# ScalarE takes the copy of the turned first-norm row before the second norm of its step

## The reference, cut to what matters

```
h = concat(token_table[x], cat_table[x])          # 64 x 128 x 256
h = h + linear_attention(layernorm(h))            # 16 heads, phi = elu + 1
h = h + moe_attention(layernorm(h))               # 16 experts, top two, then causal attention
```

## Time and profile before

| what | value |
|---|---|
| median of three runs | 983.25 us |
| the profiled execution, its own time | 981.2 us |
| its span, first to last instruction | 979.5 us |
| mean granted TensorE clock (1.0 is full speed) | 0.996 |
| PE busy | 922.2 us, 94% of the span |
| DVE busy | 843.0 us, 86% |
| POOL busy | 675.2 us, 69% |
| ACT busy | 599.7 us, 61% |

### The profile page before, as it was taken

How to read it: one execution, slowest core, us unless ns; L and a number is a source line. 1 busy time by engine, 2 the same in 40 slices (tenths; PEclk the granted TensorE clock), 3 DMA queues, 4 the chain that set the end, 5 groups by cost and what they waited for, 6 DMA issues and landing times.

```text
span 979.5 us, 20631 instructions
## 1 busy us (share of the span) xinstructions
PE 922.2 (94%) x5231; PEld 795.1 (81%) x5231; DVE 843.0 (86%) x2918; ACT 599.7 (61%) x1633; POOL 675.2 (69%) x902
## 2 busy tenths in 40 slices
PE   4999999999989999989899999999999999999998
PEld 3778788887778889889899878888888888888776
DVE  3789999999999987656575579999999999999998
ACT  4566666767666654335444556667666666666664
POOL 5437777777777755199500368888888888888885
PEclk9999999999999999999999999999999999999999
DMA  2114344443334349888988833333333333333331
GB/s 67 50 55 129 119 135 146 148 156 119 123 120 127 101 140 319 284 281 262 293 258 257 254 89 108 100 104 98 105 109 108 104 101 97 105 109 108 94 96 38
DMA packets 106298, 137.54 MB, mean 140 GB/s; under 512 B 13762, under 2 KB 93634, under 8 KB 106180
## 3 DMA queue, kind: packets, MB, share of 16 engines
q1 hardware_dynamic: 88500, 85.03, 27.6%
q0 software_dynamic: 17408, 50.35, 17.4%
q10 hardware_dynamic: 272, 0.79, 0.2%
HBM read 70.06 MB, written 66.06 MB: 139 GB/s over the span
## 4 chain that ended last, share of the span: by engine, by line
PE 38%; DVE 37%; issue 10%; POOL 7%; DMA 4%; ACT 3%; SPq 1%; DVEq 0%; POOLq 0%; ACTq 0%
PE bank L1800 10%; PE bank L1802 10%; PE bank L1801 9%; PE bank L1807 4%; DVE phi L1396 4%; DVE qk_e L1712 3%; DVE x L1712 2%; POOL row_y L924 2%; DVE attn L1339 2%; DVE kvm L1415 2%; DVE w_attn L1737 2%; DVE stats L1352 2%; PE bank L1826 2%; DVE stats L1178 2%; DVE zden L1337 1%
## 5 line engine op out<-in xcount | busy, mean ns | idle before, releaser
L1800 PE MATMUL bank<-wo_hi,split_lo 128*128 128x512 f32 x512 | 214.2, 418 | 5.1 <-issue 4.1
L1802 PE MATMUL bank<-wo_hi,split_hi 128*128 128x512 f32 x512 | 202.9, 396 | 0.0
L1801 PE MATMUL bank<-wo_lo,split_hi 128*128 128x512 f32 x512 | 202.7, 396 | 0.0
L924 POOL DMA_INDIRECT row_y<-sorted_y,pair_now x128 | 128.2, 1002 | 31.8 <-issue 22.0
L1077 ACT ACTIVATE h<-bank,rwo 128x256 f32<-128x256 f32 x256 | 107.0, 471 | 29.6 <-PE bank L1802 20.5
L1800 PEld LDWEIGHTS bank<-wo_hi,split_lo 128*128 128x128 f32 x512 | 97.1, 190 | 24.7 <-issue 4.3
L1802 PEld LDWEIGHTS bank<-wo_hi,split_hi 128*128 128x128 f32 x512 | 96.5, 189 | 23.0
L1801 PEld LDWEIGHTS bank<-wo_lo,split_hi 128*128 128x128 f32 x512 | 97.2, 190 | 17.2
L1712 DVE SCALAR_TENSOR_TENSOR qk_e<-bank,rwo,qk_e 128x256 f32<-128x256 f32 x256 | 110.9, 474 | 0.2 <-PE bank L1802 0.2
L833 POOL TENSOR_TENSOR roots<-roots_in,minus_half 128x3 f32<-128x3 f32 x67 | 59.6, 890 | 73.9 <-DVE roots_in L1361 73.9
L1800 PE MATMUL bank<-wq_hi,split_lo 128*128 x288 | 110.3, 383 | 0.0
(11 more groups left out here) (261 smaller groups left out, 2601.6 us busy)
## 6 DMA issues: line engine op xcount, KB each, us to landing
sorted_y<-w_attn SPq DMA_DIRECT2D x34, 384.0 KB, 3.6
h_rows<-h SPq DMA_DIRECT2D x64, 128.0 KB, 1.7
row_x<-h_rows SPq DMA_DIRECT2D x64, 128.0 KB, 3.6
out_h<-row_x SPq DMA_DIRECT2D x64, 128.0 KB, 2.5
sorted_y<-row_y SPq DMA_DIRECT2D x18, 384.0 KB, 3.1
h<-sorted_x SPq DMA_DIRECT2D x53, 128.0 KB, 2.9
sorted_y<-raw SPq DMA_DIRECT2D x12, 384.0 KB, 3.0
sorted_x<-zeros SPq DMA_DIRECT2D x32, 128.0 KB
```

The lines of the kernel that those rows point to most:

```text
L924: pool.indirect_dma_start(out=row_y[:, 2 * tile.p + n, :], out_offset=None, in_=sorted_y[0:LATE_FROM * P, :] if tile.c < KEPT else sorted_ ...
L1800: pe.matmul(ps, left[1][c], right[0][c], start=(c == 0), stop=False)
L1801: pe.matmul(ps, left[0][c], right[1][c], start=False, stop=False)
L1802: last = pe.matmul(ps, left[0][c], right[0][c], start=False, stop=(c == n - 1))
```

## The change

On ACT, in `step1`, the call of `second_norm` moves down behind the copy of v (line 1002), the one piece of the second stage that stands in step 60, and the copy of the turned x1 (line 1010). The order of a step becomes: qk_neg, qk_e, first norm, vx, copy of the turned x1, second norm, pqT, x2T, expert weight. No instruction, wait, buffer or engine is added, removed or changed, and the other engines' programs stay as they are.

```
                     act.activation(x1[:, :], h[t % 8], ACT.Identity, scale=roots[:, t, 0:1],
                                    bias=centers[:, t, 0:1]).then_inc(done["x1_normed"], 1)
-                if i.shift(1).inside(B):
-                    second_norm(i.shift(1))
                 tile = i.shift(3)
                 if tile.inside(B):
...
                              ).then_inc(done["v_copied"], 1)
-                if i.c == TAIL_STEP - 1:
-                    split_and_copy(Tile(-2))
                 tile = i.shift(4)
                 if tile.inside(B):
                     after(act, "x1_turned", tile)
                     after(act, "v_product", tile.shift(-1))
                     act.copy(x1T_s[0], ps_x1[:, 0:C]).then_inc(done["x1_T"], 1)
+                if i.c == TAIL_STEP - 1:
+                    split_and_copy(Tile(-2))
+                if i.shift(1).inside(B):
+                    second_norm(i.shift(1))
                 tile = i.shift(3)
```

## The result

The changed kernel takes 1035.54 us (median of four runs, 1034.16 to 1037.51), 1.0545 times the kernel before, 95% interval [1.0526, 1.0565]. It is slower by about 53 us. The forecast was slower, 1026 us in a range of 1016 to 1036; the median stands at its upper edge, and scaled by the ratio, 983.25 x 1.0545 = 1036.8 us, the result lies just above it. The mechanism was the one forecast; two of its terms had the wrong size, and two rivals, given 5% and 3%, came in part.

The account below looks back on a forecast made before the run. The first stage was taken as bound by a loop of waits through ACT, DVE and PE, 5.40 us a step. 61 x 0.70 = 42.7 plus 1.8 gave 44.5 us on 981.2, so 1026 us, range 1016 to 1036.

Parts of the forecast that it names:

- two rivals, given 5% and 3%: DVE's kvm becomes a hard wait, 15 us more, 1041 us (5%); PE's clock falls, 73 us more, 1099 us (3%).
- The step's bound, and that qk stands behind the second transpose: First stage: a 5.40 us loop of waits through three engines; PE takes the second norm's transpose, then kv, then qk.
- What the change takes away: ACT's copy of the turned x1 starts earlier, gaining 0 to 0.06 us a step, 0 to 4 us; taken as 0.
- The way to qk, 0.70 us a step: On ACT and PE, qk starts 2.91 instead of 2.20 to 2.22 us after the first norm: 42.7 us over 61 steps.
- kvm, 0.03 us a step: DVE's kvm starts 0.19 us or slightly more after qk's start, for 0.17, delaying the centers: 1.8 us in all.
- the rival's 0.25 us: If kv's result reaches DVE 0.25 us later than assumed, centers and first norm shift equally: 15 us more, 1041 us (5%).
- The clock: PE idles another 0.7 us a step, its clock falls to 1.2 GHz: 1.2 us a step, 73 us, 1099 us (3%).
- The prediction's own sign of being wrong: qk starting without a wait for line 955 ahead, first-stage granted clock under 1, or a later stage returning the time.
- No return in later stages: Second and third stages start from the first one's end and have nothing in the change that would shorten them.

Follow-up runs that it names:

- the fastest kernel: Changed kernel, but the second norm's transpose behind qk and v on PE, x2T in ACT's next step, kv ahead of the logits: 974.93 us, ratio 0.9939.

## Why the prediction was wrong, step by step

- *The step's bound, and that qk stands behind the second transpose*: right. Taking kv from between them, or the transpose out of the way, returned nine tenths or more of the loss.
- *What the change takes away*: right in that it could gain next to nothing. The copy starts 1.19 us after the first norm for 1.23; in the experiment with the transpose last it is worth 0.05 us a step, of the 0 to 0.06 given.
- *The way to qk, 0.70 us a step*: measured 0.61 to 0.63. The second norm at 1.46 (for 1.42) and the transpose at 2.21 (for 2.16) are right; the two pitches behind it were read too long, kv 0.25 for 0.28 and qk 0.37 for 0.47. That term is 61 x 0.62 = 38 us, for 42.7.
- *kvm, 0.03 us a step*: too small, and this is the first step that failed. kvm starts 0.35 us behind qk and not 0.19, partly because qk follows kv more closely and partly because DVE starts 0.11 us behind kv's end (231.28 + 0.61 to 232.00), for the 0.05 assumed. It makes plain steps, which the exponential had released, wait for the centers: 0.12 us there, 0.15 us in the mean, so 7 to 9 us for 1.8. The prediction read one step, in which the exponential releases the first norm, and said that all 61 have its shape; in the kernel before the centers already released it in 40 of them, where it starts 1.19 us or more after qk_neg, and there a later kvm is paid in full. About half of the rival's 0.25 us came, at a chance of 5%.
- *The clock*: the second step that failed, and the one that put the time above the range. The rival was priced as every step or none, 73 us, and set aside with 3% on the word of a stretch of 10.5 us at a clock of 1.00. Such a stretch shows that the clock can hold through pauses, not that it holds 61 times. The prediction's own sign of being wrong, a granted clock of this stage under 1, came: 0.97. It fell in six of 61 steps in each of two profiles, for 8.4 us in the first. The Trainium skill ("TensorE: Matmul & The Clock Gate", section "A second HAM failure mode: psum-queue depth-cycling") speaks of a clock that swings under short pauses; the trace agrees, with 0.78 to 0.81 in these steps of both profiles and 18 of them where the pause is 1.05 to 1.11 us. An expectation by share, some steps at 1.2 us each, would have put the upper end of the range higher.
- *No return in later stages*: right. The stage's 54.9 us and the span's 54.6 agree.

The errors of the way to qk (some 5 us too much) and of kvm (5 to 8 too little) nearly cancel, which is luck; most of the miss against 1026 is the clock.

## What to carry to other kernels

When an instruction is moved down one engine's order, look at its consumer's place in the other engine's order: here a transpose that nobody needed soon stood ahead of the product that everybody waited for. A step can have two ways through it with nearly the same length, and a delay on the second one (kv, kvm, roots, centers) is paid where it overtakes the first, so both have to be added up. Where a change makes TensorE pause in every step, price the lower clock as a share of the steps, and try a few idle matmuls in the pause.

## What the runs showed that was not expected

Work added to PE made the kernel faster: three matmuls in each pause took the time from 1.0545 to 1.0429 of the kernel before. They removed the steps at the lower clock, and the transpose behind them followed the second norm's start in 0.65 us and not 0.75 us; why it is sooner was not tried. Six of them did no more than three. And the second stage took 204 to 210 us in these kernels with the same program; its shortest times go with the fastest kernel, where PE's pause ahead of the third stage is over 2 us shorter, for a reason that stays open.
